# Five split tile pairs instead of four in a cross-network tower, two remainders made by GpSimd, and one factor of six products kept in PSUM

## The reference

```python
e = jnp.stack([tbl_0[ids[:, 0]], ..., tbl_31[ids[:, 31]]], axis=1)      # (1024, 32, 32)
# _cin(x=e, Ws, bs): for each layer, h = x at first
    z = jnp.einsum('bhd,bmd,ohm->bod', h, x, W.reshape(O, H, F))
    z = jax.nn.relu(z + b[None, :, None])
    if i < n_layers - 1:
        half = O // 2
        h, direct = (z[:, :half, :], z[:, half:, :])
    ...
# the sum over d of all direct parts, then:
h = jnp.concatenate([z, dense_ctx], axis=1)
h = jnp.maximum(h @ W_top1 + b_top1, 0.0)
h = jnp.maximum(h @ W_top2 + b_top2, 0.0)
y = h @ W_top3
```

## Time and profile before

| | before |
|---|---|
| median of three runs | 1158.95 us (1157.48 to 1160.01) |
| span of the profiled execution | 1162.5 us |
| TensorE busy | 1116.8 us (96%) |
| VectorE busy | 1083.0 us (93%) |
| GpSimd busy | 520.5 us (45%) |
| ScalarE busy | 458.8 us (39%) |

### The profile page before, as it was taken

One profiled execution on the slowest core, in us unless ns is written; L12 is line 12 of the kernel. 1 busy time (PEld: TensorE's weight loads), 2 busy tenths in 40 slices (PEclk: granted clock), 3 DMA queues, 4 the chain that ended last, 5 costly groups with the idle time before them and its releaser, 6 DMA issues.

```text
span 1162.5 us, 10957 instructions
## 1 busy us (share of the span) xinstructions
PE 1116.8 (96%) x3608; PEld 652.8 (56%) x3608; DVE 1083.0 (93%) x604; ACT 458.8 (39%) x383; POOL 520.5 (45%) x270
## 2 busy tenths in 40 slices
PE   0699999999999999999999999999999999999998
PEld 0355555556555555556555565555555555555554
DVE  1599999999999999999999999999999999999963
ACT  0134444333444433344444334444333444443424
POOL 6702445654445555454456544455555544450000
PEclk9899999999999999999999999999999999999999
DMA  7654543466554435555543455454445545433200
GB/s 222 200 165 129 148 136 118 108 153 162 161 139 137 126 108 143 161 161 139 132 135 106 140 161 161 139 146 128 112 129 160 161 140 160 131 123 96 55 1 0
DMA packets 63413, 154.94 MB, mean 133 GB/s; under 512 B 12753, under 2 KB 29394, under 8 KB 63394
## 3 DMA queue, kind: packets, MB, share of 16 engines
q1 hardware_dynamic: 52562, 146.98, 42.5%
q0 software_dynamic: 8192, 4.21, 3.0%
q10 hardware_dynamic: 2640, 3.50, 1.0%
HBM read 95.79 MB, written 8.39 MB: 90 GB/s over the span
## 4 chain that ended last, share of the span: by engine, by line
PE 93%; issue 2%; DVE 2%; ACTq 1%; another core or an unknown queue 1%; ACT 1%; DMA 0%; SPq 0%; DVEq 0%
PE z_ps L543 89%; PE u_ps L543 2%; PE mlp_ps L543 1%; DVE raw L450 1%; DVE prod_lo L457 1%; DVE prod L411 1%; DMA h_roll<-h_roll 0%; SPq L328 0%; ACT prod_hi L760 0%; SPq L329 0%; ACT h_roll L729 0%; ACT direct L747 0%; ACTq L713 0%; ACTq L715 0%
## 5 line engine op out<-in xcount | busy, mean ns | idle before, releaser
L543 PE MATMUL z_ps<-prod,w_sb 128*128 128x512 f32 x1536 | 692.8, 597 | 39.2 <-issue 28.4
L303 POOL DMA_INDIRECT gathered<-in_table,rows_sb x256 | 504.9, 1972 | 499.5 <-DVE h2x L464 428.8
L543 PEld LDWEIGHTS z_ps<-prod,w_sb 128*128 128x128 f32 x1536 | 292.7, 191 | 350.6 <-issue 333.8
L760 ACT CAST prod_hi<-raw 128x2048 fp32r<-128x2048 f32 x128 | 243.9, 1905 | 396.5 <-DVE raw L450 389.4
L450 DVE TENSOR_TENSOR raw<-h_roll,x_roll 128x2048 f32<-128x2048 f32 x128 | 293.1, 2290 | 5.6 <-DMA h_roll<-h_roll 2.1
L457 DVE TENSOR_TENSOR prod_lo<-raw,prod_hi 128x2048 fp32r<-128x2048 f32 x128 | 292.0, 2281 | 2.6 <-ACT prod_hi L760 2.6
L411 DVE TENSOR_TENSOR prod<-h_roll,x_roll 128x2048 f32<-128x2048 f32 x128 | 292.6, 2286 | 0.0
L543 PE MATMUL z_ps<-prod_hi,w_hi 128*128 128x512 f32 x520 | 215.4, 494 | 0.4 <-DVE prod_lo L457 0.4
L543 PE MATMUL z_ps<-prod_lo,w_hi 128*128 128x512 f32 x520 | 164.1, 395 | 0.0
L543 PE MATMUL z_ps<-prod_hi,w_lo 128*128 128x512 f32 x520 | 163.8, 395 | 0.0
L411 DVE TENSOR_TENSOR prod<-x_base,x_roll 128x2048 f32<-128x2048 f32 x63 | 143.4, 2286 | 12.8 <-DMA x_roll<-x_dram 10.8
(11 more groups left out here) (56 smaller groups left out, 240.8 us busy)
## 6 DMA issues: line engine op xcount, KB each, us to landing
x_roll<-x_dram SPq DMA_DIRECT2D x128, 512.0 KB
x_base<-x_dram SPq DMA_DIRECT2D x32, 512.0 KB
h_roll<-h_roll SPq DMA_DIRECT2D x32, 448.0 KB, 4.6
h_roll<-h_roll SPq DMA_DIRECT2D x32, 384.0 KB, 5.4
h_roll<-h_roll SPq DMA_DIRECT2D x32, 320.0 KB
x_dram<-gathered SPq DMA_DIRECT2D x64, 128.0 KB
h_roll<-h_roll SPq DMA_DIRECT2D x32, 192.0 KB
gathered<-in_table,rows_sb POOLq DMA_INDIRECT x256
```

The lines of the kernel that those rows point to most:

```text
L303: nc.gpsimd.indirect_dma_start(gathered[:, u, g * DIM:(g + 1) * DIM], None, table, bass.IndirectOffsetOnAxis(ap=rows_sb[:, col:col + 1], a ...
L543: return nc.tensor.matmul(*args, **kw)
L760: nc.scalar.copy(prod_hi[:, b % SPLIT_RING, :, :], raw[:, :, :]).then_inc(hi_ready, 1)
```

## The change

Before, eight of the 16 tiles of layer 1 are split. After, ten are. The tiles of layer 1 are named by `k` (how far h is rolled) and `b` (the shift of x). The names of the five split pairs are B0, B1, B2, B3 (k = 2 and 3, b = 0 to 3, as before) and A1 (k = 1, b = 2 and 3). Three whole pairs stay: k = 1 with b = 0 and 1 (`rolled_once`), and k = 0 with b = 0 and 1, and with b = 2 and 3.

- The k = 0 copy of h and, in turn, the next chunk's `x_base` are copied by ScalarE into `mlp_ps` (`copy_h0`, `copy_x`). The two k = 0 products and the two products of layer 0 read that factor from PSUM. `x_base` has one buffer instead of two.
- The remainders of B1 and B3 are made by GpSimd (`lo1`, `lo3`), except B3's of the last two chunks.
- GpSimd gathers chunk `c + 3` in the step of `c`, behind `lo1(c)`. `lo3(c)` comes at the head of the next step.
- `prod` has two pairs instead of three, `raw` has two buffers instead of one, `prod_hi` and `prod_lo` have three slots instead of two.
- TensorE multiplies B3 of chunk `c` between the two layer-0 pairs of the next step. SyncE's waits for a free `x_roll` follow the new order of its readers. The clearing of `top_b` and the load of the dense context move to the end of the program.

```diff
-PAIRS1 = ROLLS
-RING = 3
-SPLIT_RING = 2
+WHOLE1 = 3
+B0, B1, A1, B2, B3 = range(5)
+SPLIT1 = 5
+RING = 2
+SPLIT_SLOT = (0, 1, 2, 0, 1)
+SPLIT_RING = 3
+RAW_SLOT = (0, 1, 0, 1, 0)
+RAW_RING = 2
...
-        x_base = sb("x_base", [P, 2, CHUNK])
+        x_base = sb("x_base", [P, CHUNK])
...
-        raw = sb("raw", [P, PAIR, CHUNK])
+        raw = sb("raw", [P, RAW_RING, PAIR, CHUNK])
         prod_hi = sb("prod_hi", [P, SPLIT_RING, PAIR, CHUNK], F32R)
...
+            def gather(c, u, group):
+                made = settled(pool, group + 1)
+                freed = settled(pool, c - UNROLL + 1)
                 pool.wait_ge(ids_loaded, 32)
                 pool.wait_ge(rows_made, made)
-                for u in range(UNROLL):
-                    pool.wait_ge(ids_loaded, 32)
-                    wait(pool, h2x_ready, freed[u])
-                    for g in range(GATHERS):
-                        col = u * GATHERS + g
-                        nc.gpsimd.indirect_dma_start(
-                            gathered[:, u, g * DIM:(g + 1) * DIM], None, table,
-                            bass.IndirectOffsetOnAxis(ap=rows_sb[:, col:col + 1], axis=0),
-                        ).then_inc(gather_done[u], 16)
-            gather_group(0)
-            with pool.Fori(1, CHUNKS // UNROLL) as group:
-                gather_group(group)
+                wait(pool, h2x_ready, freed)
+                for g in range(GATHERS):
+                    col = u * GATHERS + g
+                    nc.gpsimd.indirect_dma_start(
+                        gathered[:, u, g * DIM:(g + 1) * DIM], None, table,
+                        bass.IndirectOffsetOnAxis(ap=rows_sb[:, col:col + 1], axis=0),
+                    ).then_inc(gather_done[u], 16)
...
+            def lo1(c):
+                rounded = settled(pool, c * SPLIT1 + B1 + 1)
+                behind = settled(pool, lo_count(c, B0))
+                pool.wait_ge(hi_ready, rounded)
+                pool.wait_ge(lo_ready, behind)
+                nc.gpsimd.tensor_tensor(prod_lo[:, SPLIT_SLOT[B1], :, :], raw[:, RAW_SLOT[B1], :, :],
+                                        prod_hi[:, SPLIT_SLOT[B1], :, :], ALU.subtract).then_inc(lo1_ready, 1)
+            def lo3(c):
+                rounded = settled(pool, c * SPLIT1 + B3 + 1)
+                behind = settled(pool, lo_count(c, B2))
+                pool.wait_ge(hi_ready, rounded)
+                pool.wait_ge(lo_ready, behind)
+                nc.gpsimd.tensor_tensor(prod_lo[:, SPLIT_SLOT[B3], :, :], raw[:, RAW_SLOT[B3], :, :],
+                                        prod_hi[:, SPLIT_SLOT[B3], :, :], ALU.subtract).then_inc(lo3_ready, 1)
+            def step(c, u, group):
+                if is_last(c):
+                    pool.wait_ge(x_copied, CHUNKS - 2)
+                    nc.gpsimd.memset(top_b[:, :], 0.0).then_inc(top_b_zeroed, 1)
+                if not_first(c) and pool_makes_lo3(c - 1 if isinstance(c, int) else c):
+                    lo3(c - 1)
+                lo1(c)
+                ahead = UNROLL - 1
+                if not isinstance(c, int) or c + ahead < CHUNKS:
+                    if u == 1:
+                        make_rows(group + 1)
+                    gather(c + ahead, (u + ahead) % UNROLL, group if u == 0 else group + 1)
...
+            make_rows(0)
+            for c in range(UNROLL - 1):
+                gather(c, c, 0)
+            over_chunks(pool, step)
...
+                    base_free = settled(sp, c - 2)
                     before = settled(sp, c - 1)
-                    products0_before = settled(sp, first0(c - 2) + PAIRS0)
-                    products1_before = [settled(sp, first1(c - 2) + b + 1) for b in range(ROLLS)]
+                    free = [(prod_ready, settled(sp, first1(c - 2) + 2))] * 2 + [
+                        (raw_ready, settled(sp, (c - 2) * SPLIT1 + r + 1)) for r in (B2, B3)]
...
-            def split_product(c, u, b):
+            def split_product(c, u, r):
                 s = u % 2
...
                     for a in range(PAIR, ROLLS):
                         dve.wait_ge(h1_rolled[s][a - 1], (c - s + 2) * 16)
-                wait(dve, lo_ready, c * PAIRS1 + b)
-                nc.vector.tensor_tensor(raw[:, :, :], h_roll[:, s, PAIR:2 * PAIR, :], twice(x_roll[:, s, b, :]),
-                                        ALU.mult).then_inc(raw_ready, 1)
-            def split_rest(c, b):
-                dve.wait_ge(hi_ready, c * PAIRS1 + b + 1)
-                slot = b % SPLIT_RING
-                nc.vector.tensor_tensor(prod_lo[:, slot, :, :], raw[:, :, :], prod_hi[:, slot, :, :], ALU.subtract
-                                        ).then_inc(lo_ready, 1)
+                    if not_first(c) and pool_makes_lo3(c - 1 if isinstance(c, int) else c):
+                        dve.wait_ge(lo3_ready, c)
+                    elif not_first(c):
+                        dve.wait_ge(lo_ready, lo_count(c - 1, B3))
+                elif r == B1 and not_first(c):
+                    dve.wait_ge(lo_ready, lo_count(c - 1, B2))
+                elif r == B2:
+                    dve.wait_ge(lo1_ready, c + 1)
+                elif r in (A1, B3):
+                    dve.wait_ge(lo_ready, lo_count(c, B0 if r == A1 else A1))
+                if r == A1:
+                    hs, xs = twice(h_roll[:, s, 1, :]), x_roll[:, s, PAIR:2 * PAIR, :]
+                else:
...
-                for b in range(ROLLS):
-                    split_last = b == 0 and is_first(c)
...
+                def rolled_once():
+                    dve.wait_ge(h1_ready, 2 * (c + 1))
+                    dve.wait_ge(h1_rolled[s][0], (c - s + 2) * 16)
+                    whole(first1(c), slot1(c, u), twice(h_roll[:, s, 1, :]), x_roll[:, s, 0:PAIR, :])
+                if is_first(c):
+                    rolled_once()
+                split_product(c, u, B0)
+                if not is_last(c):
+                    split_rest16(c + 1)
+                if not is_first(c):
+                    rolled_once()
+                split_product(c, u, B1)
+                split_rest(c, B0)
+                dve.wait_ge(h0_copied, c + 1)
+                for k in range(PAIRS0):
+                    whole(first1(c) + 1 + k, slot1(c, u) + 1 + k, twice(mlp_ps[:, :]),
+                          x_roll[:, s, k * PAIR:(k + 1) * PAIR, :])
+                if not_first(c):
+                    layer2(c - 1, *before)
+                    sum_direct(c - 1, *before)
+                split_product(c, u, A1)
+                split_product(c, u, B2)
+                split_rest(c, A1)
+                split_product(c, u, B3)
+                split_rest(c, B2)
+                if not pool_makes_lo3(c):
+                    split_rest(c, B3)
...
             def step(c, u, group):
+                after = c + 1, (u + 1) % UNROLL
                 if not is_last(c):
-                    layer0(c + 1, (u + 1) % UNROLL)
-                    layer0_pairs16(c + 1)
+                    layer0(*after, 0)
+                if not_first(c) and pool_makes_lo3(c - 1 if isinstance(c, int) else c):
+                    split(z1_ps, c - 1, B3, stop=True)
+                if not is_last(c):
+                    layer0(*after, 1)
                 wait(pe, h2_ready, 2 * c)
                 wait(pe, direct1_ready, c)
+                layer1(c, u, 0)
+                if not is_last(c):
+                    layer0_pairs16(c + 1)
                 if not_first(c):
                     layer2_u(c - 1, (u - 1) % UNROLL)
-                for b in range(ROLLS):
-                    whole(z1_ps, first1(c) + b, slot1(c) + b, w1_sb[:, b * PAIR:(b + 1) * PAIR, :], start=b == 0)
-                    split(z1_ps, c, b, stop=b == ROLLS - 1)
-                    if b == 3 and u == 0 and not_first(c):
-                        layer2_sum(c, group - 1)
+                split(z1_ps, c, B0)
+                layer1(c, u, 1)
+                split(z1_ps, c, B1)
+                layer1(c, u, 2)
+                split(z1_ps, c, A1)
+                if u == 0 and not_first(c):
+                    layer2_sum(c, group - 1)
+                split(z1_ps, c, B2)
+                if not pool_makes_lo3(c):
+                    split(z1_ps, c, B3, stop=True)
...
+            def round_products(c, r):
+                act.wait_ge(raw_ready, c * SPLIT1 + r + 1)
+                wait(act, split_used, used_before(c, r))
+                nc.scalar.copy(prod_hi[:, SPLIT_SLOT[r], :, :], raw[:, RAW_SLOT[r], :, :]).then_inc(hi_ready, 1)
+            def copy_h0(c, u):
+                act.wait_ge(h1_ready, 2 * (c + 1))
+                if not_first(c):
+                    act.wait_ge(prod_ready, first1(c - 1) + WHOLE1 if is_last(c) else first0(c + 1) + PAIRS0)
+                nc.scalar.copy(mlp_ps[:, :], h_roll[:, u % 2, 0, :]).then_inc(h0_copied, 1)
+            def copy_x(c):
+                act.wait_ge(x_base_loaded, (c + 1) * 16)
+                act.wait_ge(prod_ready, first1(c - 2) + WHOLE1)
```

(44 more changed lines are left out.)

150 lines of the change are left out of this document (82 added, 68 removed).

## The result

| | before | after |
|---|---|---|
| median | 1159.48 us (1157.48 to 1161.79) | 1218.42 us (1216.44 to 1219.64) |
| ratio | | 1.0503 (95% interval 1.0488 to 1.0518) |
| span of the profiled execution | 1162.5 us | 1217.3 us |

What follows compares the result with a forecast made beforehand. TensorE was taken as the bound, 33.8 us a chunk. With 29 chunks at 35.35 (+45 us) and three at TensorE's pace (-2), 1162.5 + 43 = 1205.5; the median 3.5 lower gave 1202 us, range 1137 to 1232.

Steps and rivals of the forecast that it cites:

- TensorE's gain: TensorE's matmuls: one whole pair a chunk becomes a split one, -0.65 us, so TensorE needs 33.15 us a chunk.
- PSUM as a source costs VectorE nothing and lets GpSimd work: VectorE's four products with one factor in PSUM: costed at nothing extra, with `lo1` running beside two of them.
- the rival in which products from PSUM hold GpSimd off: GpSimd remainders beside VectorE's PSUM products: each stands in VectorE's way, 40.3 us a chunk, 1348 us in all; chance 0.06.
- g: Time of one GpSimd remainder of 128x2048, in no row of the profile: taken as 4.6 us.
- The loop: GpSimd's queue and VectorE, from one remainder of B0 to the next: 34.9 us with the first gather caught; chance 0.65.
- half of all chunks at 34.9 and half at 35.8: Mix of chunks with the first gather caught under the reduction or missing it: a mean of 35.35 us.
- The row-number add: GpSimd's queue, one chunk of four: the add takes the first gather's place, so that chunk takes 35.8 us.
- the first gather was to miss the reduction one time in three: GpSimd's first gather under VectorE's reduction, margin 0.3 us: a miss in one of three remaining chunks makes them 35.8 us.
- The sum: Whole kernel: +45 us over 29 chunks, -2 over the last three, on 1162.5; the median 3.5 lower, 1202 us.
- The premise about seams: GpSimd beside VectorE instructions with two SBUF inputs: a gather waits for that instruction's end, then needs 0.8 to 0.9 us.
- VectorE's stop: VectorE ahead of `raw16` or B0, waiting for `lo3`: it stands from 21.4 to 25.4 us in each loop.
- Hidden edits: ScalarE's two copies at 1.1 us each, SyncE's loads and the ring of two: all expected to stay covered.

Runs made afterwards that it cites:

- e1: The changed kernel with four of a chunk's eight gathers moved ahead of `lo1` and four left behind it; 1145.5 us, 0.987 of the kernel before.
- e5: The changed kernel with four gathers on each side of `lo1`, and B2 also waiting for A1's completion; 1144.8 us, 0.987 of the kernel before.
- e6: The changed kernel with two gathers ahead of `lo1`, six behind, and B2 also waiting for A1's completion; 1143.7 us, 0.985 of the kernel before.
- e3: The changed kernel with the two k = 0 products reading `h_roll` in SBUF instead of its copy in PSUM; 1312.5 us in one run.
- e8: The changed kernel with one gather ahead of `lo1`, seven behind, and B2 also waiting for A1's completion; 1150.2 us, 0.992 of the kernel before.
- e2: The changed kernel with B2 on VectorE also waiting for A1's own completion, all eight gathers behind `lo1`; 1183.8 us, 1.021 of the kernel before.
- e4: The changed kernel with VectorE making the remainder of B3 in all chunks, so no `lo3` on GpSimd; 1166.7 us, 1.006 of the kernel before.

## Why the prediction was right, point by point

- **TensorE's gain.** 33.15 us a chunk forecast; 33.10 to 33.21 where nothing else is late (e1, e5, e6), with TensorE busy for 698 to 700 of 700 us in e1 and e6. Shown. Before's period was taken as 33.8 from GpSimd's first gathers of a round; counted over the whole loop it is 33.68.
- **PSUM as a source costs VectorE nothing and lets GpSimd work.** The four products take 2284 ns on average from PSUM, and the one that is left in SBUF 2283. e3 shows the second half, and the rival in which products from PSUM hold GpSimd off is refuted. The Trainium skill (SBUF — State Buffer, SBUF: two separate sides) has VectorE take the pair of ports that it shares with GpSimd only with two SBUF inputs or in a two-port mode. The trace agrees: two products around `lo1` take 4.48 us from PSUM and 8.89 from SBUF.
- **g, the price of a GpSimd remainder.** 4.6 taken from rows 3.3 to 4.9 apart; `lo1` measures 4.59 and `lo3` 4.51 us (medians). The Trainium skill (GPSIMD Engine Reference, Performance versus the Vector engine) has 4.5 for an add of this length, and the trace agrees.
- **The loop.** 34.9 forecast for a chunk whose first gather is caught, 34.30 measured: `lo3` follows the last gather without the 0.3 that I had given it, and its start comes 20.2 us after `lo1`, not 20.5. Of the other 0.3, under 0.1 is g, and the rest lies behind `lo3`: 9.6 us from its end to the next `lo1`, not 9.8. That the order in GpSimd's queue is the cause is shown by e1, which moves only gathers, and by e8 and e6, which do the same against e2.
- **The step that was mis-sized** is the mix of the kinds of chunk, "half of all chunks at 34.9 and half at 35.8", and its two reasons failed. The row-number add was to take the place of a gather in one chunk of four, 35.8 there; all seven such chunks took 34.3 to 34.4. In the rest the first gather was to miss the reduction one time in three; from the second chunk on it never did. Instead the second gather lost two seams in 16 chunks, which the forecast didn't have at all, and those took 36.8 on average. The mean came to 35.79, not 35.35. That it came so near is luck in part: the seven chunks were 10 us too high in the forecast, the other 22 together 23 us too low.
- **The sum.** Of the 16 us between forecast and result, 29 x 0.44 = 13 are the mean. The kernel before counted as 33.68 and not 33.8 adds 3.5; start and tail, 6.6 us shorter where I had 2, take off 4.6; and the median lies 1.2 us above the profiled span, not 3.5 below it, which adds 4.7. With the pause, which takes the lost seams away, the kernel is at 1183.8.
- **The premise about seams.** "Only one gather passes per such VectorE instruction" is a limit that held. I had used it as a promise too, that one does pass at each seam. That held for every gather of the kernel before (the longest is 2.95 us), but not after.
- **VectorE's stop.** 4 us a chunk forecast, 123 / 29 = 4.2 measured, a good third of it inside the busy time of `raw16`.
- **Hidden edits** (ScalarE's copies of 1.0 us, SyncE's new waits, the ring of two) stayed hidden as far as the time tells where TensorE led. In e4, where two engines are nearly level, the waits point to the ring and to `z1_ps`; the price of each stays open.

## What to carry to other kernels

When an engine that was a side hand gets work on the path, follow its whole queue round to the next release of the same work: here eight gathers stood between two subtractions, the loop was 34 to 37 us against 33.15 of matmul, and moving two of them to another place in the same queue, with the pause, turned 5% slower into 1.5% faster; moving four without it gave 1.3%. A cover made for one instruction is worth something only if that instruction can start when the cover does. Before moving the rest away too, ask who waits for what is moved: six gathers ahead of `lo1` cost 41 us against two.

## What the runs showed of the hardware

- A GpSimd instruction that asks for the shared port under VectorE instructions with two SBUF inputs, which follow each other without a pause, may lose a seam: 6.49 us and two seams for a gather that takes 0.94 alone, in 16 of 29 chunks; 8.7 us and one seam for a subtraction that takes 4.5, in 7 of 32 (e3). A pause on VectorE of 0.19 us from start to start, at the first of those seams, brought the gather to 2.08 every time. Every gather that lost had asked 1.00 to 1.03 us after A1's start; why some that asked in that window lost and others didn't stays open.
- The hold-off is exclusive in both directions and for whole instructions: `raw16` stretched from 0.42 to 3.03 us beside `lo3` (it ends 0.3 us behind it), and two products from 4.5 to 8.9 around `lo1` (e3). The profile counts it as busy time on either engine.
